# Two attention layers on one core: the eighth tile of the softmax sums added by a DMA, with sums, group statistics and loads moved to match

## What is computed

```python
xn = group_norm(x, 32 groups, gamma, beta)
qkv = einsum('bchw,oc->bohw', xn, w_qkv) + b_qkv
q, k, v = per head, 32 channels each
m = softmax(einsum('bhcs,bhct->bhst', q * scale, k * scale), axis=-1)
a = einsum('bhst,bhct->bhcs', m, v)
out = x + einsum('bchw,oc->bohw', a, w_proj) + b_proj
```

## Time and profile before

| What | Before |
|---|---|
| median of 3 runs | 2108.15 us (2107.35 to 2112.71) |
| the profiled execution's own time | 2116.79 us |
| its span | 2115.0 us |
| TensorE (PE) busy | 2080.4 us, 98% |
| VectorE (DVE) busy | 1699.9 us, 80% |
| ScalarE (ACT) busy | 1248.6 us, 59% |
| GpSimd (POOL) busy | 1781.6 us, 84% |
| mean granted TensorE clock | 0.993 of full speed |
| DMA bytes, share of the 16 DMA engines (SyncE's queue) | 152.84 MB, 31.9% |
| sums from a tile of `pt`, instructions | 552 |
| sums from `acc`, instructions | 512 |

### The profile page before, as it was taken

One profiled execution on the slowest core, in us unless ns is written; L12 is line 12 of the kernel. 1 busy time (PEld: TensorE's weight loads), 2 busy tenths in 40 slices (PEclk: granted clock), 3 DMA queues, 4 the chain that ended last, 5 costly groups with the idle time before them and its releaser, 6 DMA issues.

```text
span 2115.0 us, 31151 instructions
## 1 busy us (share of the span) xinstructions
PE 2080.4 (98%) x10568; PEld 1148.4 (54%) x10568; DVE 1699.9 (80%) x2896; ACT 1248.6 (59%) x2321; POOL 1781.6 (84%) x565
## 2 busy tenths in 40 slices
PE   6999999999999999999999999999999999999998
PEld 3455555555555555555555555555555555556543
DVE  4788888888888888888888888888887888888882
ACT  1456656565565665656556566565656656566554
POOL 2598888898888988988988888988889889889885
PEclk9899999999999999999999999999999999999999
DMA  4332233422234332244422334232343322433211
GB/s 125 61 88 48 59 88 81 100 56 68 59 81 101 76 77 52 58 100 101 100 40 62 86 81 100 58 73 58 75 100 81 80 50 52 100 81 81 49 32 40
DMA packets 208525, 156.40 MB, mean 74 GB/s; under 512 B 166512, under 2 KB 166640, under 8 KB 208368
## 3 DMA queue, kind: packets, MB, share of 16 engines
q1 hardware_dynamic: 207792, 152.84, 31.9%
q10 hardware_dynamic: 576, 1.57, 0.3%
HBM read 36.32 MB, written 16.78 MB: 25 GB/s over the span
## 4 chain that ended last, share of the span: by engine, by line
PE 93%; DVE 3%; SPq 1%; ACT 1%; issue 1%; DMA 1%; POOL 0%; ACTq 0%; DVEq 0%; POOLq 0%
PE ps_t L397 24%; PE ps_v L445 21%; PE ps_m L424 21%; PE ps_d L473 11%; PE ps_m L464 6%; PE ps_d L488 5%; PE ps_d L481 5%; DVE raw_max L728 2%; ACT pt L646 1%; SPq L304 1%; SPq L294 1%; PE ps_m L473 0%; PE ps_m L481 0%; DMA qs<-neg_max 0%; DMA par<-pars_dram 0%
## 5 line engine op out<-in xcount | busy, mean ns | idle before, releaser
L646 ACT ACTIVATE pt<-ps_t 128x512 f32<-128x512 f32 x2048 | 1122.0, 598 | 804.0 <-PE ps_t L397 796.1
L728 DVE TENSOR_REDUCE raw_max<-ps_m 128x1 f32<-128x512 f32 x2048 | 1338.1, 686 | 301.2 <-PE ps_m L424 299.0
L897 POOL TENSOR_TENSOR acc<-acc,pt 128x2048 f32<-128x2048 f32 x315 | 1441.7, 4577 | 42.9 <-ACT pt L646 1.0
L424 PE MATMUL ps_m<-ks,qs 96*128 96x512 f32 x2048 | 990.1, 484 | 7.4 <-DVE raw_max L728 5.0
L397 PE MATMUL ps_t<-qs,ks 97*128 97x512 f32 x2048 | 843.2, 413 | 1.9 <-ACT pt L646 1.1
L397 PEld LDWEIGHTS ps_t<-qs,ks 97*128 97x128 f32 x2048 | 390.1, 191 | 371.3 <-issue 224.6
L897 POOL TENSOR_TENSOR acc<-pt 128x2048 f32<-128x2048 f32 x64 | 293.0, 4579 | 238.6 <-ACT pt L646 238.6
L445 PE MATMUL ps_v<-pt,v 128*32 128x512 f32 x4096 | 492.4, 598 | 0.0
L424 PEld LDWEIGHTS ps_m<-ks,qs 96*128 96x128 f32 x2048 | 390.5, 191 | 178.6 <-DVE raw_max L728 100.9
L473 PE MATMUL ps_d<-xn,wq 128*128 128x512 f32 x500 | 263.4, 610 | 10.0 <-ACT xn L678 5.7
L445 PEld LDWEIGHTS ps_v<-pt,v 128*32 128x32 f32 x4096 | 113.6, 109 | 259.2 <-issue 183.3
(11 more groups left out here) (52 smaller groups left out, 537.5 us busy)
## 6 DMA issues: line engine op xcount, KB each, us to landing
qs<-stage_qh SPq DMA_DIRECT2D x256, 128.0 KB, 2.4
ks<-stage_kh SPq DMA_DIRECT2D x248, 128.0 KB, 2.4
qs<-stage_ql SPq DMA_DIRECT2D x128, 128.0 KB, 2.5
qs<-neg_max SPq DMA_DIRECT2D x1024, 0.5 KB, 2.0
ks<-stage_kl SPq DMA_DIRECT2D x124, 128.0 KB, 2.4
xn<-x_dram SPq DMA_DIRECT2D x16, 512.0 KB, 4.6
res<-x_dram SPq DMA_DIRECT2D x16, 512.0 KB, 4.5
between<-res SPq DMA_DIRECT2D x32, 256.0 KB, 2.3
```

The lines of the kernel that those rows point to most:

```text
L424: pe.matmul(ps_m[place % RING][:, :], qs[b][0:KROWS, h, c:c + P], ks[b][0:KROWS, h, kf * HALF:(kf + 1) * HALF], start=True, stop=True).the ...
L646: act.activation(tile_of(half, t)[:, h, :], ps_t[(UNITS * s.n + u) % RING][:, :], ACT.Exp, scale=SCALE).then_inc(exp_done, 1)
L728: dve.tensor_reduce(raw_max[:, e % 2, t, kf:kf + 1], ps_m[MAX_PLACE["max", UNITS * n + w] % RING][:, :], AX.X, ALU.max)\
L897: pool.tensor_tensor(acc[hf][:, :, :], a[:, :, :], tile_of(half, t)[:, :, :], ALU.add).then_inc(pool_added, 1)
```

## The change

1. A DMA that accumulates, issued by GpSimd, adds tile 7 into `acc` behind the six adds (`add_last_tile`), in the 61 halves before `END`. It waits for the tile's exponentials and for the sixth add, and counts `last_tile_added`.
2. In these halves `sums` runs over `acc` alone and waits for `last_tile_added`. It stands at unit 19 after the half's end instead of 11. ScalarE waits for `last_tile_added` before it writes over a tile 7.
3. `group_stats` goes from `u` = 52 of the slots with `s.g` = 1 to `u` = 7 of the slots with `s.g` = 0, into `ps_v`; the first `weighted_values` of that slot waits for `gm_done`, and dense step 6 doesn't any more.
4. `scale_and_shift` goes to the start of the slots with `s.g` = 0 on GpSimd, ahead of the first add; `mean_square` goes behind the third add; `bn_stats` and the adding of the quarters go to later units.
5. The image load goes behind the third row of a slot with `s.g` = 1 and the residual's behind the fifth.

```diff
-SUMS_AT = 11
+SUMS_AT = 19
-STATS_AT = (23, 26, 28, 33)
-GN_AT = 52
+STATS_AT = (39, 42, 44, 49)
+GN_AT = 7
...
-                    if s.g == 1 and piece == 0 and next_layer is not None:
+                    if s.g == 1 and piece == LOAD_AT and next_layer is not None:
...
-                    if s.g == 1 and piece == 1:
+                    if s.g == 1 and piece == RESIDUAL_AT:
...
                         pe.wait_ge(v_done, 4 * s.j + 4)
+                        if s.g == 0 and 0 < s.n < SLOTS - 2:
+
+                            pe.wait_ge(gm_done, s.j + 2)
...
-                    if t == POOLED_TILES:
+                    if t == ALL_BUT_LAST:
+
+                        pe.wait_ge(last_tile_added, 16 * (half + 1))
+                    elif t == POOLED_TILES:
...
-                        if s.g == 1 and s.n + 3 < SLOTS and step == STATS_BEFORE:
-
-                            pe.wait_ge(gm_done, s.j + 3)
-                        elif r:
+                        if r:
...
-                            sums(half, (*range(pooled_in(half), NT), POOLED_TILES))
+                            if half < END:
+                                sums(half, (ALL_BUT_LAST,))
+                            else:
+                                sums(half, (*range(pooled_in(half), NT), POOLED_TILES))
...
-                    if s.g == 1 and has_third and u == GN_AT:
-
-                        pe.wait_ge(qkl_done, 4 * (s.n + 2) + STATS_BEFORE - 4)
-                        group_stats(s.j + 2, ps_d)
+                    if s.g == 0 and has_second and not first and u == GN_AT:
+
+                        pe.wait_ge(raw_done, NH * s.n)
+                        group_stats(s.j + 1, ps_v)
...
                         act.wait_ge(pool_added, added(old, max(1, k)))
+                    elif old < END:
+                        act.wait_ge(last_tile_added, 16 * (old + 1))
...
-                    if s.g == 1 and has_third and u == GN_AT + LATER:
-                        group_stats_out(s.j + 2, ps_d)
+                    if s.g == 0 and has_second and not first and u == GN_AT + LATER:
+                        group_stats_out(s.j + 1, ps_v)
...
-                    if s.g == 1 and has_third and u == GN_AT - 1:
+                    if s.g == 1 and has_third and u == QUARTERS_AT:
...
+            def add_last_tile(half, hf):
+
+
+                pool.wait_ge(exp_done, HG * (NT * half + NT))
+                pool.wait_ge(pool_added, added(half, POOLED - 1))
+                pool.dma_start(acc[hf][:, :, :], tile_of(half, POOLED)[:, :, :], accum_op=ALU.add).then_inc(last_tile_added, 16)
+
...
+                if s.g == 0 and has_second and not first:
+                    scale_and_shift(s.j + 1, 1 - s.v)
...
-                        if s.g == 1 and has_third and hf == 1 and t == 1:
+                        if s.g == 1 and has_third and hf == 1 and t == 3:
                             mean_square(s.j + 2)
-                        if s.g == 1 and has_third and hf == 1 and t == 4:
-                            scale_and_shift(s.j + 2, s.v)
+                    if NH * s.n + hf < END:
+                        add_last_tile(NH * s.n + hf, hf)
...
+LOAD_AT, RESIDUAL_AT = 2, 4
+QUARTERS_AT = 60
```

More of the change, by code:

```diff
@@ L246, in attention_layers @@
         pool_added = sem("pool_added")
+        last_tile_added = sem("last_tile_added")
         sum_ready = sem("sum_ready")
@@ L926 @@
 LAST_OUT = 5
+LOAD_AT, RESIDUAL_AT = 2, 4
+QUARTERS_AT = 60
 LAST_SUMS_AT = 59
 LAST_KT0_AT = 60
-STATS_BEFORE = 6
-POOLED_TILES = -1
+POOLED_TILES, ALL_BUT_LAST = -1, -2
 _OUT = (B, C, 32, 32)
```

## The result

| | Before | After |
|---|---|---|
| median | 2108.24 us (4 runs) | 2064.55 us (2059.56 to 2069.11, 4 runs) |
| ratio | | 0.978, 95% interval 0.9764 to 0.9797 |
| profiled execution, span | 2116.79, 2115.0 us | 2059.56, 2057.8 us |
| one block in the steady part | 128.04 us | 124.87 us |

By these medians the kernel is 43.7 us faster. The forecast was 2067. The ratio is estimated from the single runs and is not the quotient of the two medians: 0.978 of 2108.24 us is 46 us less. So the gain is about 47 us, and the medians of the table put it somewhat low.

What follows compares the result with a forecast made beforehand. TensorE, busy for 98% of the span and streaming, was taken as the bound. Sums -53.7, group statistics -5.6 and VectorE's +18.1 gave -41.2 us, 2108.15 to 2067; likeliest range 2046 to 2088 (0.70), high end 2120.

Steps and rivals of the forecast that it cites:

- TensorE streams, so a tile less is 0.88 us less: Sums on TensorE: 61 of 64 halves lose one tile of 0.88 us, 53.7 us gained, all on the chain.
- Group statistics, 0.4 us per block: Moved small matmul no longer waits for ScalarE's copy: 0.4 us, between 0.29 and 0.78, in 14 images, 5.6 us gained.
- VectorE gives 18.1 us back: Waits for VectorE's divisions behind the earlier-ending sums take back 9.3, 2.8 and 6.0 us, together 18.1.
- the 0.3 us for each first half: Third maximum matmul behind the sums waits for the division: 0.3 us in each of 31 first halves, 9.3 us.
- with `bn_stats`: A `bn_stats` at unit 49, two units ahead of the division, adds 0.2 us in 14 slots, 2.8 us.
- the dense step at unit 22: Output projection's third piece, three units behind the sums at 19, waits 0.4 us for the division, 15 times: 6.0 us.
- An issue costs GpSimd 1.2 us: Each of 61 DMA issues takes GpSimd 1.2 us, between 0.6 and 4.7; up to 2.3 it doesn't set the pace.
- The transfer lands after 8.4 us, within 6.2 to 10.5: Accumulating DMA of tile 7 lands 8.4 us after issue; 11.2 us available for landing, 8.0 behind scale and shift.
- the half behind scale and shift: Half whose adds end some 3.2 us later, leaving 8.0 us for landing, which the forecast 8.4 meets.
- Rows of maxima are delayed by little, loads cost nothing: SyncE's row DMAs beside the transfer: little delay, engines half free beside heads; loads behind third and fifth group cost nothing.
- The sum: Whole kernel: -53.7 - 5.6 + 18.1 = -41.2 us, so the median goes from 2108.15 to 2067.

Runs made afterwards that it cites:

- e8_second_issue: Changed kernel with a second accumulating DMA, of 16 columns into a tile of its own, behind each of the 61; median 2076.13 us, ratio 0.9828.
- e3_plain_copy: Changed kernel with its DMA copying tile 7 over acc instead of adding, and the exponential's scale a thousandth; 2064.17 us, one run.
- the second measurement: The unaltered changed kernel measured again beside the kernel before: 2064.69 us against 2112.39, ratio 0.9775.

## Why the prediction was right, step by step

- **TensorE streams, so a tile less is 0.88 us less.** Right: 4 x 31.77 us of a block would be 4 x 30.89 without any wait, 3.52 less. In 61 halves that is 53.7 us.
- **Group statistics, 0.4 us per block.** The mechanism was right, the size too small: the term was mis-sized. The eight units with the small matmul cost 0.78 us more than others and cost 0.20 more now, so the move is worth 0.58 per block, 8.1 us in 14 where 5.6 was forecast. The named wait of 0.29 was only half of it.
- **VectorE gives 18.1 us back.** The mechanism was right, the size too large. Over its free 4 x 30.89 us the block has 1.31 us of waits and small pieces, before it had 0.96 over 4 x 31.77. With the 0.58 that the group statistics gave, that makes 0.93 us given back per block, some 14 us, where 1.2 was forecast. The term that was mis-sized is the 0.3 us for each first half: where no `bn_stats` stands ahead it is 0.07. The reading behind it was wrong: the prediction took it that the division starts when its predecessor ends, at 1004.33, and so can't start earlier when the sums get shorter. But the division of before started at 1004.43, 0.14 behind the end of its own sums (1003.25 + 1.04 = 1004.29); they were what it waited for. The maxima ahead of it start as far behind the sums now as then (980.55 to 981.84, 1002.37 to 1003.65), and the division starts 0.59 us after them (982.43) instead of 0.78. The other sizes held: with `bn_stats` 0.41 against 0.5, the dense step at unit 22 0.37 against 0.4 (0.47 with what follows, by the period of 31.36).
- **An issue costs GpSimd 1.2 us.** It is 1.4, of which 0.85 is the issue itself; far from the 2.3 that GpSimd has free, as `e8_second_issue` confirms from the other side.
- **The transfer lands after 8.4 us, within 6.2 to 10.5.** It is 8.8 in the median, 7.6 with little beside it, 10.3 beside staged heads. The bounds held for the median; nine of the 61 took longer than 10.5, the longest 10.9. The page of the Trainium skill (DMA: Bandwidth & Descriptors, Anatomy of one DMA) gave an estimate of 4.4 us for the copy and 6.8 for both operands. The trace shows 5.8 and 8.8 in the median, so here the rates from rows were nearer. In the third half of a block, where no heads are on their way beside it, the copy of `e3_plain_copy` took 4.7 us in the median, near the 4.4 of the Trainium skill, and the accumulating DMA 7.8. What the prediction left out is that landing differs by stretch: it called the half behind scale and shift the critical one (median of the spare time 1.2 us), and the tightest is the second half of a block, whose DMA meets the heads (0.7).
- **Rows of maxima are delayed by little, loads cost nothing.** Right in the result and for a reason that was too simple. The DMA does slow SyncE's issues, nearly threefold at most, and the loads' new place is what hides it.
- **The sum.** 3.17 us per block x 15 is some 47 us by the trace, 47.7 in the second measurement, 43.7 by the medians of the first, 41.2 by the forecast. With the measured sizes the forecast's own sum is -53.7 - 8.1 + 14 = -48. So the sum missed 6 to 7 us of gain: a give-back taken 4 us too large and a move taken 2.5 too small, both on the same side. That 2064.55 lies only 2.5 us from 2067 is in part luck of the runs. That the DMA costs nothing, on which the forecast stood, is what the runs showed.

## What to carry to other kernels

When one engine streams without gaps, a matmul taken away is worth its spacing in the timeline, and the work lies in naming who is next: here a division, an issue and a landing, each with its spare time counted from the row where it starts to the row that needs it. A DMA that adds can take over work from a full engine for 1.4 us of GpSimd and, for this 1 MB, 7.2 to 10.9 us of latency, if its reader stands further back than that. And look at the queues beside it: the cost that counted most, 22 us, would have come from DMAs that the change had moved out of the way.

## What the hardware showed that was not expected

- **An accumulating DMA slows the issues of another queue.** Of 237 groups of four row DMAs that begin between 100 and 1950 us, 21 took over 5 us to issue in the changed kernel (longest 6.92), where 2.46 is usual. All 21 are among the 66 that began with the accumulating DMA on its way; of the other 171 the longest took 3.59. Before it was none of 231 (longest 3.97), with a plain copy in its place one of 237 (longest 5.24), with no DMA none of 237 (longest 3.68). Why it does so, no run here shows.
- **Accumulating doubles the engines' time** (8.2% to 15.9% for the same 64 MB) and adds 3 us to the landing: as much as a second copy, not half of one as I had assumed.
- **An issue on GpSimd costs about the same for 1 MB and for 8 KB**, 0.8 to 0.85 us with 144 packets either way, and only once per group the 0.55 us of standing idle behind the add ahead.
- Three sums of the changed kernel's profiled execution wait for the DMA, by 0.16 to 0.38 us. Their DMAs landed 10.1, 10.4 and 10.3 us after issue, where the same half of a block has 7.8, 9.6 and 9.6 in the median. Why these landed late was not settled; it is under 1 us in all.
